# Softmax blocks of sizes of their own in three GAT passes, and tables of steps for the work behind them

## The reference

```python
for m in range(3):
    h = x @ W[m]
    e = (h @ a_src[m])[src] + (h @ a_dst[m])[dst]     # edges and one self loop per node
    e = leaky_relu(e, 0.2)
    w = exp(e - segment_max(e, dst)[dst])
    alpha = w / segment_sum(w, dst)[dst]
    x = x + sigmoid(segment_sum(alpha * h[src], dst) + b[m])
```

## Time and profile before

| | |
|---|---|
| median of 3 executions | 6016.25 us (6013.4 to 6020.16) |
| the profiled execution | 6015.73 us, of which the span of its instructions is 6014.0 us |
| DVE busy over the span | 72% |
| PE busy over the span | 84% |
| POOL busy over the span | 59% |
| attention pass 0, first dots to last scan | 2129 to 2604 us |
| attention pass 1 | 2622 to 3214 us |
| attention pass 2 | 3217 to 3847 us |

### The profile page before, as it was taken

The page is one execution under the profiler, slowest core; times in us unless marked ns, Lnnn a source line. Parts: engine busy times, 40 slices in busy tenths (PEclk is TensorE's granted clock), DMA queues, the critical chain, the costliest instruction groups (busy, mean ns, idle before and its releaser), DMA issues. The chain is left out here.

```text
span 6014.0 us, 100399 instructions
## 1 busy us (share of the span) xinstructions
PE 5078.0 (84%) x23996; PEld 3008.8 (50%) x23996; DVE 4339.4 (72%) x11924; ACT 3405.6 (57%) x7493; POOL 3537.2 (59%) x3533
## 2 busy tenths in 40 slices
PE   4999999999994768847884888799989997777775
PEld 2666666666652235424442444466656664333332
DVE  7988888888874899958885999566645555544453
ACT  4888888888874956735663577533323333222222
POOL 3544444444421657437764775277767765777777
PEclk9999999999997977967886999899999999999998
DMA  9999997777655857736664899677667774444442
GB/s 218 308 302 299 303 299 240 244 244 238 230 189 168 290 172 214 206 118 187 203 198 128 265 294 284 204 219 218 215 210 234 234 220 146 133 130 130 132 131 80
DMA packets 909508, 1274.03 MB, mean 212 GB/s; under 512 B 248502, under 2 KB 398967, under 8 KB 902579
## 3 DMA queue, kind: packets, MB, share of 16 engines
q1 hardware_dynamic: 696170, 1063.92, 54.0%
q0 software_dynamic: 112896, 202.19, 13.9%
q10 hardware_dynamic: 100016, 3.20, 1.3%
HBM read 623.49 MB, written 654.07 MB: 212 GB/s over the span
## 5 line engine op out<-in xcount | busy, mean ns | idle before, releaser
L1738 POOL DMA_INDIRECT n_xs<-table,look x1176 | 1197.8, 1019 | 558.8 <-issue 349.8
L1439 POOL DMA_INDIRECT g_xs<-table,look x784 | 775.8, 989 | 454.1 <-issue 233.6
L1877 DVE TENSOR_TENSOR_SCAN n_dT<-n_km,n_dT,bank 128x512 f32<-128x512 uint8 x291 | 372.3, 1279 | 496.1 <-PE bank L1765 493.3
L626 POOL DMA_INDIRECT p_rows<-in_x_dram,dst_ix x392 | 390.4, 996 | 487.5 <-DMA raw_rows<-p_rows 264.7
L634 POOL DMA_INDIRECT table<-slot_pair,map_ix x392 | 397.1, 1013 | 454.5 <-ACT n_sg L742 247.7
L670 PE MATMUL bank<-n_xT,gat_w 128*128 128x512 f32 (+1 forms) x1176 | 545.2, 599 | 18.4 <-ACT n_xT L734 16.3
L689 PE MATMUL bank<-n_zT,wn 128*128 128x512 f32 (+1 forms) x1176 | 537.1, 592 | 6.6 <-ACT n_zT L734 6.6
L1750 POOL DMA_INDIRECT out_dram<-n_xn,n_row_of x392 | 385.5, 983 | 140.0 <-issue 118.5
L1557 ACT ACTIVATE g_xw<-g_xs,g_cols 128x128 f32<-128x128 f32 x1176 | 370.7, 387 | 76.1 <-PE bank L1507 49.0
L1859 ACT ACTIVATE n_xn<-bank 128x512 f32<-128x512 f32 x98 | 58.4, 596 | 624.8 <-DMA out_dram<-n_xn,n_row_of 624.8
L865 DVE COPY n_ro<-bank 128x512 f32<-128x512 f32 (+1 forms) x392 | 256.4, 685 | 197.3 <-PE bank L699 134.4
(11 more groups left out here) (278 smaller groups left out, 12574.7 us busy)
## 6 DMA issues: line engine op xcount, KB each, us to landing
table<-n_ro SPq DMA_DIRECT2D x768, 256.0 KB
g_gb<-decays SPq DMA_DIRECT2D x294, 256.0 KB
n_xd<-table SPq DMA_DIRECT2D x294, 256.0 KB
table<-g_xn SPq DMA_DIRECT2D x196, 256.0 KB
g_xo<-table SPq DMA_DIRECT2D x196, 256.0 KB
edge_feats<-n_eT SPq DMA_DIRECT2D x196, 256.0 KB
table<-n_xn SPq DMA_DIRECT2D x196, 256.0 KB
n_ea<-edge_feats SPq DMA_DIRECT2D x196, 256.0 KB
```

Of the source, the lines that this page charges most:

```text
L626: q.indirect_dma_start(out=edge_rows[e % UX][:, u, :], out_offset=None, in_=x, in_offset=bass.IndirectOffsetOnAxis(ap=dst_ix[:, t:t + 1], ...
L1439: q.indirect_dma_start(out=xs[g % XR][:, u, :], out_offset=None, in_=tables[l], in_offset=bass.IndirectOffsetOnAxis(ap=src_ix[:, t:t + 1] ...
L1738: q.indirect_dma_start(out=xs.buffers[g % UE][:, u, :], out_offset=None, in_=tables[L], in_offset=bass.IndirectOffsetOnAxis(ap=look[:, t, ...
L1877: V.tensor_tensor_scan(in_order(dT[g][:, :]), kept(g), in_order(flat_banks[1]), 0.0 if begins(g) else carry(dT[g.before(1)]), ALU.mult, AL ...
```

## The change

The block of 7 groups gives way to a list of sizes for each pass, and the lag of 16 to a table of steps.

```diff
+SIZES = [[5, 9] + 5 * [14] + [9, 5], [5] + 12 * [7] + [5, 4], [5] + 9 * [9] + [7, 5]]
+QUICK = [GE, 82, GE]
+NORM_SIZES = 13 * [7] + [4, 3]
...
-            for s in range(groups + max(lag for lag, _ in work)):
-                for lag, fn in work:
-                    if 0 <= s - lag < groups:
-                        fn(s - lag)
+            work = [([g + lag for g in range(groups)] if isinstance(lag, int) else lag, fn) for lag, fn in work]
+            for s in range(1 + max(steps[-1] for steps, _ in work)):
+                for steps, fn in work:
+                    for g in range(groups):
+                        if steps[g] == s:
+                            fn(g)
...
-            ends = [(S_ + 1) * SG - 1 for S_ in range(GE // SG)]
-            XR, OR = FIRST if l == 0 else 20, 9
+            sizes = SIZES[l]
+            begins = [sum(sizes[:k]) for k in range(NBL + 1)]
+            ends = [b - 1 for b in begins[1:]]
+            SB = max(sizes)
...
+            def step_behind(ready_at, quick):
+                steps, at = [], 0
+                for g in range(GE):
+                    at = max(3 * ready_at(g), at + (2 if g >= quick else 3))
+                    steps.append(-(-at // 3))
+                return steps
+
+            scale_at = step_behind(lambda g: ends[block_of[g]] + 10, QUICK[l])
+            def later(n):
+                return [s + n for s in scale_at]
+            normal_at = step_behind(lambda g: scale_at[norm_ends[norm_of[g]]] + 9, GE)
+            XR, OR = FIRST if l == 0 else SB + 13, 12 if l == 1 else 9
...
-                cols = of_ring(f"g{l}_cols", 2, (P, 2, ST), c=c2)
+                cols = of_ring(f"g{l}_cols", 3, (P, 2, ST), c=c2)
...
-                            elif g == SG + 3:
+                            elif g == sizes[0] + 3:
                                 q.wait_ge(vb, marks["columns", 0])
...
-                        flat(GE, [(7, weights), (16, scale)] + ([(23, join)] if last_layer else [(20, add_half)]) + [(21, gate)]
-                             + ([(31, normalise)] if last_layer else [(23, copy_back), (24, copy_dots)]))
+                        flat(GE, [(7, weights), (scale_at, scale)] + ([(later(7), join)] if last_layer else [(later(4), add_half)])
+                             + [(later(5), gate)]
+                             + ([(normal_at, normalise)] if last_layer else [(later(7), copy_back), (later(8), copy_dots)]))
```

More of the change, by code:

```diff
@@ L1092, in gat_pass, with rows, tiles @@
                 junk = of_ring(f"g{l}_junk", 2, c=c2)
-                ST = SG * U
+                ST = SB * U
+                def rows(s):
+                    return sizes[s] * U
+                def tiles(s):
+                    return slice(begins[s] * U, begins[s + 1] * U)
                 zz = of_ring(f"g{l}_zz", 2, (P, ST), c=c2)
@@ L1185, in max_carry @@
                                 v.wait_ge(far_ld, 16)
-                            step(V.tensor_tensor_scan(mc[:, s * ST + 1:(s + 1) * ST + 1], tf[:, s * ST:(s + 1) * ST],
-                                                      banks[6][0:1, 1, 0:ST], mc[:, s * ST:s * ST + 1], ALU.add, ALU.max))
+                            t = tiles(s)
+                            step(V.tensor_tensor_scan(mc[:, t.start + 1:t.stop + 1], tf[:, t], banks[6][0:1, 1, 0:rows(s)],
+                                                      mc[:, t.start:t.start + 1], ALU.add, ALU.max))
                             marks["max_carry", s] = n_seg[0]
@@ L1220, in sum_carry @@
                                 return
-                            s, k = g // SG, g // SG % 2
+                            s, k = block_of[g], block_of[g] % 2
                             v.wait_ge(pb, 6 * s + 4)
-                            step(V.tensor_copy(pc[k][:, :], banks[6][0:1, 3, 64:64 + ST]))
+                            n, t = rows(s), tiles(s)
+                            step(V.tensor_copy(pc[k][:, 0:n], banks[6][0:1, 3, 64:64 + n]))
                             seen()
-                            step(V.tensor_tensor_scan(lc[:, s * ST + 1:(s + 1) * ST + 1], pc[k][:, :], banks[6][0:1, 3, 0:ST],
-                                                      lc[:, s * ST:s * ST + 1], ALU.mult, ALU.add))
+                            step(V.tensor_tensor_scan(lc[:, t.start + 1:t.stop + 1], pc[k][:, 0:n], banks[6][0:1, 3, 0:n],
+                                                      lc[:, t.start:t.start + 1], ALU.mult, ALU.add))
                             marks["sum_carry", s] = n_seg[0]
@@ L1584, in weights @@
                                 a.wait_ge(pb, 6 * (s - 1))
-                            S.activation(ex[k][:, :, :], ev[k][:, :, :], ACT.Exp).then_inc(ab, 1)
+                            n = rows(s)
+                            S.activation(ex[k][0:n, :, :], ev[k][0:n, :, :], ACT.Exp).then_inc(ab, 1)
                         def copy_back(g):
```

176 lines of the change are left out of this document (97 added, 79 removed).

## The result

The changed kernel takes **6049.32 us** (median of 5, 6045.06 to 6060.97) against 6017.2 for the kernel before on the same chip. The ratio is 1.0052, with a 95% interval from 1.004 to 1.0064. It is slower by 32 us, where I had forecast 26 us faster. The profiled execution took 6048.1 us with a span of 6046.0.

A forecast was written before the change was run, and what follows sets the result against it. It took DVE to bound pass 0's middle and pass 2, POOL pass 1. Gains of 12, 6 and 8 us, 26 in all, off the span of 6014.0 give 5988, plus 1.7: 5990 us, range 5968 to 6007.

The forecast's parts named there:

- DVE's price for the first part: Pass 1's drain, last dots to columns: four softmax steps with 1.5 groups of 2.83 us each plus 7.6, 24.6 us.
- the 8 us that I had: Pass 1's drain: last scale 8 us earlier; 2 go for work piling up ahead of step 102, leaving 6 us.
- the 3.38 us: PE's own time for a group at full clock; pass 0's drain was forecast as 45.2 + 7 x 3.38 = 68.9 us.
- bounds 0 (pairs wait on each other in rings of 2 and 3): Pass 1's low bound: groups sharing a step wait on each other, gain 0 instead of 6 us; upper bound 16.
- a sign of error: Pass 1's drain: the prediction is wrong if pairs take more than 5 us a step.
- the ring of pass 0: Pass 0: rows held up to 23 steps slow the gathers; at 5.97 a group 12 us slower, 6028; chance 0.04.
- The free case: Pass 0: last dots 53.8 us earlier, at 2497, before any costs are set against it.
- the two gaps: Pass 0, steps 19 to 22 and 32 to 36, nothing scaled: 10 us for PE's clock, 5 for uncovered round trips.
- the tie: Pass 0, steps 37 to 102: DVE and the gathers, limited by 32 slots, both need 275 us; costs 3 us more.
- the rival of the free gaps: Trailing work keeps PE's clock, gathers run at 5.1: pass 0 gains 27, in all 41, 5975 us; chance 0.17.
- my 4.5 us a step: Pass 2's drain: 49.5 us for 11 steps before, 58.5 for 13 after, last scale 6.6 us earlier.
- The wait of 1.84 us: End of pass 2: ACT's wait for the last scales goes, covered by normalising six groups at 1.6 us each.

The follow-up runs named there:

- thirds from group 82 on: Changed kernel with lags in thirds of a step, pass 1's quick groups two thirds apart, never two in one step: 6018.94 us, ratio 1.0002.
- the same, pass 2 in blocks of 7: Changed kernel with pass 1's quick groups two thirds of a step apart, pass 2 in 14 blocks of 7, last normalisation's end changed: 6015.33 us, ratio 0.9996.
- thirds from the last dots on: As thirds from group 82 on, but pass 1's quick part begins with group 86: 6005.63 us, one execution.
- The kernel with less PE work: The kernel with the moved calculation, but pass 1's last 19 groups form the next layer's scalars for 128 of 512 edges: 5988.7 us, one execution.
- the same pairs, one by one: Changed kernel, but a step with two groups runs the whole list for the first group, softmax included, then for the second: 6021.19 us, one execution.
- the kernel with pass 0 alone: Changed kernel's sizes kept only in pass 0; passes 1 and 2 back to 14 blocks of 7, no pairs: 5993.6 us, ratio 0.9963.
- The kernel with the moved calculation: Kernel with the graded blocks and pass 2 up to 9, but no calculation of scales in steps 102 to 106: 5997.1 us, one execution.
- the graded blocks: Kernel before with pass 0 in ten growing and shrinking blocks: 5996.95 us, ratio 0.9968; with pass 2 in blocks up to 9, 5996.52 us.

## Why the prediction was wrong

**What pass 1's drain is bound by: this step failed, and with it the sign.** I counted "4 x 1.5 x 2.83 + 7.6 = 24.6" us from the last dots to the columns, "only three more groups ahead of the last at 3.38", together 34.7 us to the last `scale`, and let the end of the pass follow at the old distance. Measured:

| | dots to columns | columns to last scale | last scale to the end | sum |
|---|---|---|---|---|
| before | 18.9 | 23.9 | 26.2 | 69.0 |
| forecast | 24.6 | 10.1 | unchanged | 61 |
| pairs (the change) | 41.1 | 25.9 | 45.0 | 112.0 |
| thirds from group 82 on | 23.9 | 17.5 | 34.2 | 75.6 |
| the same, pass 2 in blocks of 7 | 27.3 | 18.8 | 34.2 | 80.2 |
| thirds from the last dots on | 23.7 | 16.9 | 38.4 | 79.0 |

Where no two groups share a step, DVE's price for the first part was about right. What stands behind it was wrong in every order: I had put the growth of the last part at nothing. Work that is packed closer on ACT does not leave PE sooner. Busy time of the kernel before in the whole drain, then up to the last `scale` and behind it, and PE's whole group at full clock:

```profile
3148.00:3214.00 66.00, 62.53 (x324) 34.08 (x322) 50.43 (x115) 51.68 (x117) 0.00 (x0) 0.96 0.53 166
3148.00:3191.00 43.00, 41.54 (x222) 23.91 (x220) 41.01 (x101) 35.18 (x86) 0.00 (x0) 0.94 0.66 198
3191.00:3214.00 23.00, 20.99 (x104) 10.17 (x103) 9.42 (x15) 16.50 (x33) 0.00 (x0) 1.00 0.29 104
```

```profile
3186.98 0.66 PE L1507 MATMUL bank<-ident,g_xw 128*128 128x128 f32 x4
3187.57 0.38 PE L1514 MATMUL bank<-brow,ones 3*128 3x512 bf16 x1
3187.89 1.16 PE L1517 MATMUL bank<-gat_w,g_acc 128*128 128x128 f32 x8
3188.88 0.60 PE L1538 MATMUL bank<-ident,g_xn 128*128 128x128 f32 x4
3189.41 1.02 PE L1544 MATMUL bank<-g_nT,v_own 128*2 128x512 f32 x2
3190.36 0.66 PE L1507 MATMUL bank<-ident,g_xw 128*128 128x128 f32 x4
```

PE is busy 62.5 of 66 us. When the last dots run, in step 102, `dot` stands at group 78, and `turn` at 84. So 13 `turn`, 15 `multiply`, 18 `turn_back` and 19 `dot` are left. By the starts above (0.59, 1.31, 0.53 and 0.95 us) they are 55 us at full clock; the transposes of the last softmax and stretches at half clock make up the rest of the 62.5. PE's idle time is 3.5 us. Scaling earlier could gain at most that and what the lower clock cost: by my estimate 2.6 us, half of the some 5 us at half clock that a mean of 0.96 over 66 us makes. That is under the 8 us that I had. At the last `scale` 9 products (`dot`) are left before, and 13 with thirds from the last dots on: the table moved groups forward on ACT and put them in a queue before PE. The kernel with less PE work confirms it for the part behind the last `scale`. Up to the last `scale` DVE (41.0 of 43 us busy) is as full as PE, and no run shows which of them sets the pace there. I knew the 3.38 us and used it for pass 0's drain, but did not ask what was left for PE.

**The ring of waits: the size of a named bound.** I wrote "bounds 0 (pairs wait on each other in rings of 2 and 3)", and pass 1 lost 44 us. I had allowed for pairs that fill no gap, not for pairs that hold up the softmax queued behind them. The runs divide the 44 us: the order within the step is 19 (the same pairs, one by one), two groups in one step against an even pace is 26 in all, quickening before the last dots is about 7 (613.1 against 606.4), and 11 are left when thirds begin late. Each of these terms rests on differences of single executions, which vary by some 4 us. The last 11 stand behind the last `scale` (38.4 us in place of 26.2), where 13 products are left for PE and not 9. From the last dots to its last product PE was idle for 10.6 of 76 us, against 3.6 of 66 before; what causes that stays open. I had named as a sign of error that pairs would take more than 5 us a step, and no rival had it; my one slower rival was the ring of pass 0, which did not come.

**Pass 0: right mechanism, sized too small.** Last dots came 46 us earlier where I had 36 (2550.9 to 2515). The free case gave 53.8, so the two gaps and the tie cost 8 together and not 18. The drain took 67.4 us, for which I had 68.9. The gain is 24 by this pair of executions and 22 by the kernel with pass 0 alone, in place of 12, between forecast and the rival of the free gaps. The gaps cost little because DVE had the trailing work: 39.0 of 40 us busy, as the stretch above shows. For the clock I had the rule of the Trainium skill's TensorE: Matmul & The Clock Gate, HAM oscillation, by which stretches of matmuls that are short against the waits between them each start cold. In the second gap PE was not in that case, and the trace says nothing against the rule: PE was idle 5.3 of 24.8 us, 2.0 us at most at a time, and the granted clock was 1.00 up to 2239; only 6.8 us of half clock came afterwards, behind an idle piece of 3.0 us. In the first gap the clock was 0.50 all through, 7.6 us longer than before, with PE busy 21.4 of 26 us and DVE 23.0; what that cost by itself no run shows. The tie with the ring was a good guess: POOL did stop once for the ring (8.84 us), and at the end the dots stood 9 us behind the gathers.

**Pass 2: DVE's saving was real, and two costs ate it.** Two fewer blocks and two fewer groups were to bring the last dots 15.6 us forward; they came 8.0 forward in this pair of executions, and 12 by the means of five kernels with blocks of 7 and seven with blocks of 9 (538.5 and 526.7). The start of the last gather, at 503.6, would have allowed 513. In the stretch shown above DVE lost 8.5 us more to gathered rows (15.4 against 6.9) and 4.8 to PE, for which I had put 4 in all. The drain I put at 58.5 us and it took 65.2. The kernel with the moved calculation took 58.7. So my 4.5 us a step was right, and the missing part is one calculation of scales that fell among the steps of the last softmax: I had placed it "into the drain, where ACT and PE set the pace", but there DVE is in the chain. The wait of 1.84 us did go. Altogether the blocks of 9 bring nothing, and cost some 3 us by the means: 629.5 to 633.9 us in five kernels with blocks of 7, 632.6 to 636.6 in seven with blocks of 9, and 630.1 and 631.4 in the two with the calculation moved.

**The version that beats both.** Pass 0 alone: 5993.6 us, 0.37% below the kernel before. That the graded blocks or the moved calculation of scales bring anything on top of it was not shown; they were within the noise.

## What to carry to other kernels

Before a drain is reordered, count for each engine what it still has to do from the point where the bound ends: if one engine is busy 95% of it, no order makes it much shorter. Carry the sum to the end of the pass and not to the last start of the stage that was moved: with thirds from the last dots on, the last `scale` came 2 us sooner behind the last dots than before, and the end of the pass 10 us later. When a table puts two items in one step of an in-order queue, look up what each second item waits for and what stands queued behind it. If that includes something the releasing engine needs first, the two waits add up step after step. Delay of consumers is cheap as long as the bounding engine has other work: pass 0 went without scaling for 24 to 27 us twice and gained 24 us.

## What was not expected of the hardware

The granted clock did not fall in the second gap of pass 0, though nothing was scaled for 25 us: the transposes and products of that time left PE idle for 5.3 us, in pieces of 2.0 us at most. In pass 1's drain the clock was 0.83 on average from 3126 to 3226, with PE busy 68% and four idle pieces of 2.9 to 4.0 us in front of `turn`. The four gathers of a group take 5.0 us when POOL does not stop (mostly 0.95 and 0.30 us each). Over the last 66 groups of pass 0 the mean is 5.37 us, with one stop of 8.84 us in it, and DVE is busy 97% of 2190 to 2500. So the two engines are now a near tie; the graded sizes ended the gathers 5 us earlier and the dots only 1 us.
